# The second stream of batches runs half a period behind the first in the last stage of a four-stage network

## The chip, the cores and the metric

The kernel runs on one core of one Trainium2 chip. The metric is device time in microseconds of the whole program. Engines are named as in the profile: PE (TensorE, its weight loads are PEld), DVE (VectorE), ACT (ScalarE), POOL (GpSimd), SP (the queue that issues most transfers).

## The reference

Four blocks follow one another on an activation of 4 batches x 1024 tokens x 128 channels: a Mamba block, a top-2 mixture of experts, a differential attention, and a last block, which the change touches. The last block normalizes twice, gates 8 attention experts, sums their q, k and v projections weighted by the gate, makes one causal attention of it, projects with 8 weighted output matrices, normalizes, gates 8 experts of a second mixture, and normalizes once more:

```python
logits = normalize(flat_hs) @ normalize(sim) - sigmoid(gates)   # then mask and softmax: weight of each of 8 experts
q, k, v = sum over e of w_e * (h @ q_proj[e]), w_e * (h @ k_proj[e]), w_e * (h @ v_proj[e])
h = h + sum over e of w_e * (softmax(causal(q k^T)) v @ o_proj[e])
h = h + sum over e of m_e * (gelu(layernorm(h) @ w1[e]) @ w2[e])
```

Each block's output is layer-normalized and added to its input. (The lines above are shortened from the reference; E = 8, hidden size 128.)

## The kernel before

Each engine has one instruction queue that it works through in order. Work of different batches is interleaved when the program is written out: every part is a Python generator that yields a due time ahead of each piece, and `weave` always takes the stream with the smallest due time. The due times (tables `D_LN`, `D_TR`, `D_GATE`, `D_ATT`, `D_OUT`, `D_MOE` with `D_PERIOD` and `D_EXPERT`) never reach the chip; they only fix the order in each queue. What really holds an instruction back are semaphores.

The last stage has two streams. Stream k = 0 does batches 0 and 2, stream k = 1 batches 1 and 3; each has its own PSUM banks (stream 0 has `ps0` and `ps1`, stream 1 has `ps2` and `ps3`) and its own buffers. Before the change both streams have the same due times, so that every piece of stream 1 stands right behind the same piece of stream 0. One batch (index r in a stream) goes through these parts, with due times from the start of its period of 177.2:

- **Normalizations and first gate** (0 to 24). `stats` (8 x BN_STATS, 8 x BN_AGGR on DVE), `rstd` on POOL, `norms` on DVE, the same again with `affine`; transposes on PE, copies to `xT` on ACT, `logits` on PE (L1586), gate arithmetic on DVE (L1323 to L1347), an exponential on ACT (L1506), the weights on DVE (L1352 to L1358).
- **Projection steps** q = 0..15 (24 to 76). POOL scales the tile (L1476), PE transposes it (L1597), ACT and DVE split it into a high and a low half (L1521, L1380), PE multiplies with q and k weights (L645 to L647, six products of 512 columns) and with the v weights (L1648, 12 products). Behind step 7 and step 15 ACT copies q, k and v out (L1526 to L1529).
- **Attention rows** i = 0..7 (76 to 110). PE scores (L1608), DVE mask and maximum (L1394, L1396), ACT exponential (L1536), PE transposes (L1668), ACT copies (L1544), PE output (L1678), DVE scaling by the row's sum (L1386, piece `weighed`). The scores of row i + 1 wait for the exponential of row i.
- **Head steps** j = 0..7 (111 to 126). Two PE products of 512 columns (L1696), then eight additions in a chain on DVE (L1410).
- **Second normalization and gate** (125 to 142), as above.
- **Expert steps** x = 0..15 (142 to 171). PE up (L1711), ACT Gelu (L1557), PE down (L1724), DVE four additions (L1430).
- **Last normalization** (171 to 177), its sum into `X` on POOL (L1484), and the store.

Ahead of both streams stand `experts_act`, `experts_dve`, `experts_pool` and `experts_pe`: they prepare the gate matrices and split the q, k and v weights, loaded in this stage as `raw`, into two fp16 halves (three copies on ACT at L1267, three subtractions on DVE at L1285).

Of the kernel before, what the change touches and what calls it, by code (L numbers as in the profile page):

```python
# [104 lines left out]
def program(nc, d, out):  # L105
    ctx = ExitStack()
    with ctx:
# [1078 lines left out]
        D_PERIOD, D_EXPERT = 177.2, 3.15  # L1186
# [6 lines left out]
        def d_at(r, t):  # L1193
            return D_PERIOD * r + t

        def d_scaled(r, q):

            h, x = q // 8, q % 8
            return d_at(r, 24 + 26.2 * h if x == 0 else 25 + 26.2 * h + D_EXPERT * (x - 1))

        def d_proj(r, q, more=0.0):
            return d_at(r, 25 + 26.2 * (q // 8) + D_EXPERT * (q % 8) + more)
# [57 lines left out]
        def experts_act(e):  # L1260
            e.wait_ge(phase, 8)
            e.wait_ge(*t_dsp.at(0))
            e.activation(lsq[:, 16:32], bank[0][:, 0:16], ACT.Copy, scale=1.0).then_inc(*a_dsp.up("sq"))
            e.activation(flat(sgm[:, :, :]), flat(gts[:, :, :]), ACT.Exp, bias=0.0, scale=-1.0).then_inc(*a_dsp.up("exp"))
            e.wait_ge(s_wq, 16)
# [4 lines left out]
        def experts_dve(e):  # L1270
            e.wait_ge(phase, 8)
# [4 lines left out]
            e.reciprocal(sgm[:, :, :], sgm[:, :, :]).then_inc(*v_dsp.up("sgm"))  # L1276
            e.wait_ge(*p_dsp.at(0))
# [5 lines left out]
            for a in range(3):  # L1283
                e.wait_ge(*a_dsp.at(a))
                e.scalar_tensor_tensor(out=flat(wqkv3[:, 1, a, :, :]), in0=raw[:, 1024 * a:1024 * a + 1024], scalar=WS,  # L1285
                                       in1=flat(wqkv3[:, 0, a, :, :]), op0=ALU.mult, op1=ALU.subtract).then_inc(*v_dsp.up(a))

        def experts_pool(e):
            e.wait_ge(phase, 8)
# [3 lines left out]
        def experts_pe(e):  # L1293
            e.wait_ge(phase, 8)
# [3 lines left out]
        def soft_dve(e, k):  # L1298
# [17 lines left out]
            def gating(r, w, times):  # L1316
                which = w // 2
                yield d_at(r, times[1])
                e.wait_ge(*p_dln[k].at(r, w, "sq"))
                e.tensor_reduce(G(7)[:, :, 0:1], s_sq[k], AX, ALU.add).then_inc(*v_dgt[k].up(r, w, "sumsq"))  # L1320
                yield d_at(r, times[2])
# [27 lines left out]
                yield d_at(r, times[3])  # L1349
# [11 lines left out]
            for r in range(2):  # L1361
                b = k + 2 * r
                yield d_at(r, D_LN[0][0])
                stats(e, s, [tile_of(b, j) for j in range(8)], {}).then_inc(*v_dln[k].up(r, 0, "stats"))
                yield d_at(r, D_LN[0][1])
                e.wait_ge(*p_dln[k].at(r, 0, "rstd"))
                norms(e, s, [tile_of(b, j) for j in range(8)], hs).then_inc(*v_dln[k].up(r, 0, "out"))
                yield d_at(r, D_LN[1][0])
                stats(e, s, hst, {0: v_dln[k].at(r, 0, "out")}).then_inc(*v_dln[k].up(r, 1, "stats"))
                yield d_at(r, D_LN[1][1])  # L1370
# [5 lines left out]
                for q in range(16):  # L1376
                    yield d_scaled(r, q)
# [12 lines left out]
                for i in range(8):  # L1390
                    yield d_at(r, D_ATT[i])
# [8 lines left out]
                    yield d_at(r, D_ATT[i] + 1.5)  # L1400
# [3 lines left out]
                yield d_at(r, D_ATT[8])  # L1404
                weighed(7)
                for j in range(8):
                    yield d_at(r, D_OUT + 1.8 * (j + 1))
# [8 lines left out]
                yield d_at(r, D_LN[2][0])  # L1416
                stats(e, s, hst, {0: v_dom[k].at(r, 7)}).then_inc(*v_dln[k].up(r, 2, "stats"))
                yield d_at(r, D_LN[2][1])
# [3 lines left out]
                for x in range(16):  # L1422
                    yield d_at(r, D_MOE + 1.6 * (x + 2))
# [10 lines left out]
                yield d_at(r, D_LN[3][0])  # L1434
                stats(e, s, hst, {0: v_dm[k].at(r, 15)}).then_inc(*v_dln[k].up(r, 3, "stats"))
                yield d_at(r, D_LN[3][1])
# [5 lines left out]
        def soft_pool(e, k):  # L1442
# [9 lines left out]
            for r in range(2):  # L1452
                b = k + 2 * r
                yield d_at(r, D_LN[0][0])
                root(r, 0)
                for w in (0, 2):
                    yield d_at(r, D_LN[w // 2 + 1][0])
                    root(r, w // 2 + 1)
                    yield d_at(r, D_GATE[w // 2][0])
                    e.wait_ge(*v_dln[k].at(r, w // 2 + 1, "out"))  # L1460
                    e.tensor_tensor(s_sq[k], n1, n1, ALU.mult).then_inc(*p_dln[k].up(r, w, "sq"))
                    yield d_at(r, D_GATE[w // 2][2])
# [4 lines left out]
                    for q in range(16):  # L1467
                        h, x = q // 8, q % 8
                        yield d_scaled(r, q)
# [9 lines left out]
                yield d_at(r, D_LN[3][0])  # L1479
                root(r, 3)  # L1480
                yield d_at(r, D_LN[3][1])
# [4 lines left out]
        def soft_act(e, k):  # L1486
# [21 lines left out]
            for r in range(2):  # L1508
                yield d_at(r, D_TR[0])
                turned(r, 0)  # L1510
                yield d_at(r, D_GATE[0][2])
                gate(r, 0)
                for q in range(16):
                    h = q // 8
                    yield d_scaled(r, q)
# [6 lines left out]
                    if q % 8 == 7:  # L1522
                        yield d_proj(r, q, D_EXPERT)
# [7 lines left out]
                for i in range(8):  # L1531
                    yield d_at(r, D_ATT[i])
# [5 lines left out]
                    yield d_at(r, D_ATT[i] + 1.5)  # L1538
# [7 lines left out]
                yield d_at(r, D_TR[1])  # L1546
                turned(r, 1)
                yield d_at(r, D_TR[2])
                turned(r, 2)
                yield d_at(r, D_GATE[1][2])  # L1550
                gate(r, 2)
                for x in range(16):
                    yield d_at(r, D_MOE + 1.6 * x)
# [5 lines left out]
        def soft_pe(e, k):  # L1559
# [51 lines left out]
            for r in range(2):  # L1611
                yield d_at(r, D_TR[0])
                turn(r, 0)
                yield d_at(r, D_GATE[0][2])
                logits(r, 0)
                for q in range(16):
                    h, x = q // 8, q % 8
                    if x == 0:
                        yield d_scaled(r, q)
                        scaled(r, q)  # L1620
                    yield d_proj(r, q)
# [228 lines left out]
```

## Time and profile before

| | |
|---|---|
| Median of 3 runs | 3174.92 us (3171.91 to 3175.52) |
| The profiled execution: its time, its span | 3170.2 us, 3168.4 us |
| Busy share of the span: PE, DVE, ACT, POOL | 76%, 73%, 53%, 40% |
| Last stage (first instruction on DVE to the end of the last sum into X) | 2500.8 to 3160.1 us |
| Mean granted TensorE clock | 0.866 |

The span is the profiled part of an execution. The last stage is the last fifth of it, and its two periods (r = 0 and r = 1) repeat each other. A granted clock of 1.00 is 2.4 GHz and 0.50 is 1.2 GHz.

### The profile page before, as it was taken

The numbers are of one execution on the slowest core, as the hardware profiler recorded it, in microseconds if no ns is written. First come the engines' busy times: TensorE is split into PE (matmuls) and PEld (weight loads), VectorE is DVE, ScalarE is ACT, GpSimd is POOL, SyncE is SP. The second block draws the span as 40 slices with busy tenths as digits, with TensorE's granted clock in tenths as the row PEclk, the third lists the DMA queues.
The fourth block names the chain that finished last, engine by engine and source line by source line (L and its number), as shares of the span: only waits on it lengthen the run. The fifth ranks groups of instructions, "written<-read, shape, count | busy, mean of one in ns | idle before, by whom it ended". The sixth has DMA issues, their size and how long they took to land.

```text
span 3168.4 us, 41094 instructions
## 1 busy us (share of the span) xinstructions
PE 2407.0 (76%) x14962; PEld 1690.2 (53%) x14962; DVE 2311.8 (73%) x4141; ACT 1678.5 (53%) x2552; POOL 1263.5 (40%) x1203
## 2 busy tenths in 40 slices
PE   3114776667676696899999999999999388667867
PEld 1002444344344564577777777776777366245635
DVE  3994798699599612688878878887888533874386
ACT  4223663665376242678777877787778124022402
POOL 0341143144124200365766576667667540114011
PEclk8556878888788898799999999999999789788978
DMA  3000000000000000100000100010000100000000
GB/s 99 0 0 0 0 1 1 1 1 1 1 1 1 1 1 14 41 21 21 24 21 21 28 21 21 24 29 21 21 21 1 40 1 1 0 14 1 1 0 14
DMA packets 32026, 41.96 MB, mean 13 GB/s; under 512 B 8897, under 2 KB 18130, under 8 KB 31442
## 3 DMA queue, kind: packets, MB, share of 16 engines
q1 hardware_dynamic: 31826, 39.34, 4.6%
q8 instruction: 120, 1.97, 0.3%
q14 instruction: 80, 0.66, 0.1%
HBM read 12.05 MB, written 2.10 MB: 4 GB/s over the span
## 4 chain that ended last, share of the span: by engine, by line
PE 46%; DVE 20%; issue 18%; POOL 11%; ACT 4%; SPq 1%; DMA 1%; POOLq 0%; DVEq 0%; ACTq 0%
PE ps L954 10%; PE ps L932 6%; PE ps L943 6%; POOL MA L379 5%; PE ps L710 3%; DVE MA L1090 3%; DVE MA L1410 3%; PE ps L914 2%; DVE lnb L265 2%; PE ps L1724 2%; PE ps L645 2%; PE ps L1711 2%; PE ps L647 1%; PE ps L646 1%; PE ps L1648 1%
## 5 line engine op out<-in xcount | busy, mean ns | idle before, releaser
L1090 DVE TENSOR_REDUCE MA<-ps 128x1 f32<-128x1024 f32 x512 | 623.1, 1220 | 190.4 <-PE ps L932 177.6
L379 POOL TENSOR_TENSOR MA<-MA,BIG 128x1024 f32<-128x1024 f32 x120 | 280.1, 2355 | 624.3 <-DVE BIG L350 624.3
L954 PE MATMUL ps<-MA,WB 128*64 128x128 f32 x4096 | 504.5, 277 | 0.0
L954 PEld LDWEIGHTS ps<-MA,WB 128*64 128x64 f32 x4096 | 442.8, 137 | 88.4 <-issue 87.4
L344 DVE TENSOR_TENSOR_SCAN BIG<-BIG 128x1024 f32<-128x1024 f32 x128 | 346.8, 2748 | 0.0
L932 PE MATMUL ps<-BIG 96*128 96x512 f16 x1024 | 312.6, 387 | 13.3 <-DMA BIG<-WB 4.9
L632 ACT ACTIVATE HR<-ps,b 128x512 f32<-128x512 f32 x288 | 191.5, 686 | 244.0 <-PE ps L647 243.0
L710 PEld LDWEIGHTS ps<-WB,HR 128*128 128x128 f32 x2304 | 305.8, 209 | 25.0 <-issue 8.7
L710 PE MATMUL ps<-WB,HR 128*128 128x128 f32 x2304 | 312.8, 294 | 0.0
L1017 ACT ACTIVATE WB<-ps,MA 128x1024 f32<-128x1024 f32 x206 | 229.5, 1114 | 149.3 <-DVE MA L1090 147.5
L497 PE MATMUL ps<-bc,sel 96*128 96x512 bf16 x256 | 108.2, 520 | 249.1 <-DVE BIG L350 190.7
L1024 ACT ACTIVATE MA<-ps 128x1024 f32<-128x1024 f32 x256 | 259.8, 1015 | 4.9 <-PE ps L943 4.9
L436 ACT ACTIVATE BIG<-MA,aneg 128x1024 f32<-128x1024 f32 x128 | 141.5, 1142 | 109.9 <-DVE BIG L344 105.8
L1017 ACT ACTIVATE MA<-ps,MA 128x1024 f32<-128x1024 f32 x153 | 170.6, 1115 | 44.8 <-DVE MA L1090 44.8
L497 PEld LDWEIGHTS ps<-bc,sel 96*128 96x128 bf16 x256 | 22.2, 113 | 302.2 <-DVE BIG L350 213.0
L1147 POOL TENSOR_TENSOR MA<-MA 128x2 f32<-128x2 f32 x128 | 25.0, 195 | 365.2 <-DVE MA L1094 365.2
L943 PE MATMUL ps<-ident,WB 128*128 128x128 f32 x1232 | 166.1, 279 | 5.6 <-POOL WB L1159 2.5
L943 PEld LDWEIGHTS ps<-ident,WB 128*128 128x128 f32 x1232 | 144.4, 144 | 44.4 <-DVE WB L1099 10.8
L645 PE MATMUL ps<-xT,WB 128*128 128x512 f16 x288 | 126.5, 439 | 52.4 <-ACT HR L632 48.3
L248 POOL TENSOR_SCALAR st_d<-st_d 128x8 f32<-128x8 f32 x16 | 4.3, 269 | 402.6 <-DVE st_d L260 402.5
L589 DVE SCALAR_TENSOR_TENSOR acc<-ps,g,acc 128x128 f32<-128x128 f32 x256 | 71.0, 337 | 123.2 <-PE ps L710 123.2
L340 DVE TENSOR_TENSOR BIG<-MA,ps 128x1024 f32<-128x1024 f32 x128 | 149.6, 1207 | 1.2 <-PE ps L497 1.2
(286 smaller groups left out, 5133.2 us busy)
## 6 DMA issues: line engine op xcount, KB each, us to landing
BIG<-BIG SPq DMA_DIRECT2D x192, 64.0 KB, 2.0
BIG<-WB SPq DMA_DIRECT2D x192, 64.0 KB, 2.0
WB<-w_dram SPq DMA_DIRECT2D x1, 2304.0 KB, 14.6
X<-x_dram SPq DMA_DIRECT2D x4, 512.0 KB, 12.5
HR<-w_dram SPq DMA_DIRECT2D x1, 2048.0 KB, 9.3
out_dram<-X SPq DMA_DIRECT2D x4, 512.0 KB, 3.2
WB<-wqkv_dram SPq DMA_DIRECT2D x1, 1536.0 KB, 6.1
WB<-w_dram SPq DMA_DIRECT2D x2, 512.0 KB, 8.2
```

Of the source, the lines that this page charges most:

```text
L340: e.tensor_tensor(db[k][c], du[:, c, :], ps[0][:, :], ALU.mult).then_inc(*v_mtb.up(b, n, c))
L344: e.tensor_tensor_scan(db[k][c], da[k][c], db[k][c], 0.0, ALU.mult, ALU.add).then_inc(*v_mscan.up(b, n, c))
L379: e.tensor_tensor(yy[:, c, :], yy[:, c, :], db[n % 2][c], ALU.add).then_inc(*p_my.up(b, n, c))
L632: e.activation(hr[(4 * k + f) % 8], bank[4 + f % 2], ACT.Gelu, bias=small["b1"][:, PLAN[k][1], f:f + 1], scale=BACK).then_inc(*a_fg.up(b, ...
L645: e.matmul(o, w[0], x[0], start=first, stop=False)
L710: i = e.matmul(o, hr[(4 * kk + f) % 8][:, 128 * j:128 * j + 128], w2[:, x, f, :], start=f == 0 and x != 8, stop=f == 3)
L932: x = e.matmul(ps[s][:, 512 * h:512 * h + 512], stack[q % 2][0:96, 0, 2 * pp + s, 128 * i:128 * i + 128], stack[q % 2][0:96, 1, 2 * pp + s ...
L943: x = e.transpose(ps[2][:, 128 * k:128 * k + 128], P_of(n, 0)[:, 128 * k:128 * k + 128], ident[:, :])
L954: x = e.matmul(bank[6][64 * pp:64 * pp + 64, 0:128], V[(4 * b + g) % 2][:, k, 64 * pp:64 * pp + 64], DT[n % 2][:, 128 * k:128 * k + 128], ...
L1017: e.activation(P_of(n, s), ps[s][:, :], ACT.Exp, bias=L[:, 2 * s + pp:2 * s + pp + 1], scale=1.0, accum_out=L[:, 4 + 2 * s + pp:5 + 2 * s ...
L1024: e.activation(DT[n % 2], ps[2][:, :], ACT.Copy, scale=1.0).then_inc(*a_at.up(n))
L1090: e.tensor_reduce(L_of(n)[:, c:c + 1], ps[s][:, :], AX, ALU.max, negate=True).then_inc(*v_amx.up(n, s))
```

## The change

Stream 1 gets a shift `D_SHIFT` = 88.0 on all its due times, about half of the period of 177.2. Its first half (normalizations, projections) now stands among the second half (attention rows, head steps, experts) of a batch of stream 0, and the other way round. The `experts_*` functions become streams of their own with due times: the gate preparation stands partly behind the first statistics, and the three weight splits of DVE stand at 13.2, 16.7 and 20.2. No instruction of the computation is added or removed; only the order in the queues changes. (ACT table loads are placed by the compiler where the function's table changes in the queue.)

```diff
-        D_PERIOD, D_EXPERT = 177.2, 3.15
+        D_PERIOD, D_EXPERT, D_SHIFT = 177.2, 3.15, 88.0
...
-        def d_at(r, t):
-            return D_PERIOD * r + t
+        def d_at(k, r, t):
+            return D_PERIOD * r + D_SHIFT * k + t
...
         def experts_dve(e):
-            e.wait_ge(phase, 8)
+            yield 0.2
             e.tensor_tensor(lsq[:, 0:16], sims, sims, ALU.mult).then_inc(*v_dsp.up("sq"))
...
             e.reciprocal(sgm[:, :, :], sgm[:, :, :]).then_inc(*v_dsp.up("sgm"))
+            yield 7.5
             e.wait_ge(*p_dsp.at(0))
...
             for a in range(3):
+                yield 13.2 + 3.5 * a
                 e.wait_ge(*a_dsp.at(a))
...
-            experts_dve(e)
-            weave(soft_dve(e, 0), soft_dve(e, 1))
+            e.wait_ge(phase, 8)
+            weave(experts_dve(e), soft_dve(e, 0), soft_dve(e, 1))
```

The other engines change in the same way (`experts_act` yields 0.3 and 8.5, `experts_pool` 6.0, `experts_pe` 0.3), and every `d_at`, `d_scaled` and `d_proj` gets the stream's k. Line numbers behind L1183 rise by up to 3: L1380, L1410, L1506 and L1557 of before are L1383, L1413, L1509 and L1560 after the change.

On DVE, at the start of the stage, the queue before the change is this (L1278 to L1282 prepare the gate matrix, L1285 are the splits, `st_d0` and `st_d1` are the statistics of the two streams):

```order
L1272 TENSOR_TENSOR lsq<-sims 128x16
L1274 TENSOR_SCALAR sgm<-sgm 128x16
L1276 RECIPROCAL sgm<-sgm 128x16
L1278 TENSOR_SCALAR lsq<-lsq 128x16
L1280 RECIPROCAL lsq<-lsq 128x16
L1282 TENSOR_TENSOR simn<-sims,lsq 128x16
L1285 SCALAR_TENSOR_TENSOR WB<-WB 128x1024 x3
L256 BN_STATS st_d0<-X 128x6 x8
L260 BN_AGGR st_d0<-st_d0 128x2 x8
L256 BN_STATS st_d1<-X 128x6 x8
```

and after it this:

```order
L256 BN_STATS st_d0<-MA 128x6 x8
L260 BN_AGGR st_d0<-st_d0 128x2 x8
L1280 TENSOR_SCALAR lsq<-lsq 128x16
L1282 RECIPROCAL lsq<-lsq 128x16
L1284 TENSOR_TENSOR simn<-sims,lsq 128x16
L265 TENSOR_SCALAR MA<-MA,st_d0 128x128 x8
L1313 TENSOR_TENSOR MA<-MA,lnp 128x1024
L1316 TENSOR_TENSOR MA<-MA,lnp 128x1024
L1288 SCALAR_TENSOR_TENSOR WB<-WB 128x1024
L1323 TENSOR_REDUCE BIG<-BIG 128x8
L1288 SCALAR_TENSOR_TENSOR WB<-WB 128x1024
L1326 TENSOR_SCALAR BIG<-BIG 128x8
```

Only stream 0 starts here now; the gate preparation stands between its second statistics and its second normalization, and the splits (L1288) stand between pieces of its gate.

On DVE, around the second normalization, the queue before has the head steps of both streams in turn (L1410), then both statistics:

```order
L1410 SCALAR_TENSOR_TENSOR MA<-ps2,BIG,MA 128x128 x8
L1410 SCALAR_TENSOR_TENSOR MA<-ps1,BIG,MA 128x128 x8
L256 BN_STATS st_d0<-MA 128x6 x8
L260 BN_AGGR st_d0<-st_d0 128x2 x8
L1410 SCALAR_TENSOR_TENSOR MA<-ps3,BIG,MA 128x128 x8
L256 BN_STATS st_d1<-MA 128x6 x8
```

After the change, here in the part where stream 1 does its second half and stream 0 its first, the same place reads:

```order
L1413 SCALAR_TENSOR_TENSOR MA<-ps2,BIG,MA 128x128 x8
L1383 SCALAR_TENSOR_TENSOR BIG<-ps1,BIG 128x512
L1413 SCALAR_TENSOR_TENSOR MA<-ps3,BIG,MA 128x128 x8
L256 BN_STATS st_d1<-MA 128x6 x8
L260 BN_AGGR st_d1<-st_d1 128x2 x8
L1383 SCALAR_TENSOR_TENSOR BIG<-ps1,BIG 128x512
L265 TENSOR_SCALAR MA<-MA,st_d1 128x128 x8
L1313 TENSOR_TENSOR MA<-MA,lnp 128x1024
L1316 TENSOR_TENSOR MA<-MA,lnp 128x1024
L1383 SCALAR_TENSOR_TENSOR BIG<-ps1,BIG 128x512 x2
L1323 TENSOR_REDUCE BIG<-BIG 128x8
```

The low halves of stream 0's projection steps (L1383) now stand between stream 1's head steps and behind its normalization blocks.

On ACT, the queue before goes from the copies of the last projection step to the attention rows of both streams, with no table load between them:

```order
L1526 ACTIVATE MA<-ps0 128x512
L1527 ACTIVATE MA<-ps0 128x512
L1529 ACTIVATE MA<-ps1 128x512
L1536 ACTIVATE WB,BIG<-ps0,BIG 128x128
L1526 ACTIVATE MA<-ps2 128x512
L1527 ACTIVATE MA<-ps2 128x512
L1529 ACTIVATE MA<-ps3 128x512
L1536 ACTIVATE WB,BIG<-ps2,BIG 128x128
```

After the change, at the end of stream 0's expert steps (L1560, Gelu) and the start of stream 1's rows (L1539, the exponential):

```order
L1560 ACTIVATE HR<-ps0 128x512 x4
L1529 ACTIVATE MA<-ps2 128x512
L1530 ACTIVATE MA<-ps2 128x512
L1532 ACTIVATE MA<-ps3 128x512
L1539 ACT_TABLE_LOAD
L1539 ACTIVATE WB,BIG<-ps2,BIG 128x128
L1560 ACT_TABLE_LOAD
L1560 ACTIVATE HR<-ps0 128x512
L1547 ACTIVATE BIG<-ps3 128x128
L1560 ACTIVATE HR<-ps0 128x512
L1539 ACT_TABLE_LOAD
L1539 ACTIVATE WB,BIG<-ps2,BIG 128x256
```

The tail of one stream's Gelus is now mixed with the first two exponentials of the other, with three table loads among them; the whole stage has 13 table loads after the change, where it had 3.

## Rows read from the trace of the kernel before

**Rows 1.** The page's first line.

```profile
span 3168.4 us, 41094 instructions
```

**Rows 2.** Chain that ended last, by time: start us, length us, what.

```profile
2500.77 6.12 DMA WB<-wqkv_dram
2506.91 1.06 ACT WB L1267
2508.00 3.49 DVE WB L1285 x3
2511.49 1.57 DVE st_d L256 x8
...
2555.18 0.43 PE ps L645
```

**Rows 3.** Same chain: period, expert steps, last sum.

```profile
2737.86 1.66 DVE st_d L256 x8
...
3100.50 1.78 PE ps L1724 x16
...
3104.00 1.78 PE ps L1724 x16
...
3157.77 2.34 POOL X L1484
```

**Rows 4.** Busy time in stretches: PE, PEld, DVE, ACT, POOL (xinstructions), clock, DMA, GB/s.

```profile
2832.00:3157.00 325.00, 239.55 (x1464) 164.22 (x1464) 197.62 (x732) 78.39 (x150) 68.16 (x59) 0.85 0.01 4
...
2884.00:2964.00 80.00, 75.64 (x690) 52.94 (x688) 21.20 (x34) 23.58 (x45) 26.02 (x25) 1.00 0.01 1
2964.00:3012.00 48.00, 41.09 (x250) 30.62 (x251) 20.86 (x58) 23.24 (x54) 0.00 (x0) 1.00 0.00 1
3012.00:3066.00 54.00, 36.55 (x90) 14.86 (x88) 44.80 (x142) 2.06 (x4) 1.34 (x2) 0.89 0.00 0
3066.00:3096.00 30.00, 16.96 (x56) 12.52 (x56) 26.35 (x127) 4.11 (x7) 9.53 (x7) 0.52 0.00 0
3096.00:3146.00 50.00, 49.27 (x282) 35.88 (x283) 30.46 (x114) 18.28 (x32) 0.00 (x0) 1.00 0.00 1
```

**Rows 5.** Timeline, second normalization and gate: start, length, instruction, idle before.

```profile
3062.17 1.64 DVE L256 BATCH_NORM_STATS2 st_d<-MA 128x6 f32<-128x128 f32 x8
...
3064.91 1.68 POOL L250 TENSOR_TENSOR st_d<-st_d,half 128x8 f32<-128x8 f32 x1
...
3069.70 2.11 DVE L265 TENSOR_SCALAR MA<-MA,st_d 128x128 f32<-128x128 f32 x8
...
3073.10 1.23 DVE L1313 TENSOR_TENSOR MA<-MA,lnp 128x1024 f32<-128x1024 f32 x1
...
3082.29 6.83 PE L1586 MATMUL ps<-simn,xT 128*128 128x8 f32 x32
...
3085.82 0.22 DVE L1328 TENSOR_TENSOR BIG<-ps,BIG 128x64 f32<-128x64 f32 x1 [1.32 <-PE ps L1586]
...
3089.75 0.22 DVE L1347 TENSOR_TENSOR BIG<-BIG 128x64 f32<-128x64 f32 x1
...
3094.78 1.28 ACT L1557 ACT_TABLE_LOAD   x1
```

**Rows 6.** Groups by line and shape, 2832 to 3157 us: busy us, mean ns.

```profile
L1380 DVE SCALAR_TENSOR_TENSOR BIG<-ps,BIG 128x512 f16<-128x512 f32 x32 | 22.0, 691 | 54.4 <-ACT BIG L1521 54.4
L1521 ACT ACTIVATE BIG<-ps 128x512 f16<-128x512 f32 x32 | 19.0, 600 | 50.6 <-PE ps L1597 50.6
...
L265 DVE TENSOR_SCALAR lnb<-MA,st_d 128x128 f32<-128x128 f32 x20 | 7.4, 440 | 0.1
...
L1536 ACT ACTIVATE WB<-ps,BIG 128x1024 f32<-128x1024 f32 x2 | 2.2, 1110 | 1.8 <-DVE BIG L1396 1.8
```

**Rows 7.** Timeline, first head steps of the second period.

```profile
3014.62 8.11 PE L1696 MATMUL ps<-WB,xT 128*128 128x512 f32 x18
...
3017.63 12.58 DVE L1410 SCALAR_TENSOR_TENSOR MA<-ps,BIG,MA 128x128 f32<-128x128 f32 x34 [4.23 <-PE ps L1696]
```

More of the change, by code:

```diff
@@ L1191, in program, with d_scaled, d_proj @@
         D_OUT, D_MOE = 111, 142.4
-        def d_at(r, t):
-            return D_PERIOD * r + t
-        def d_scaled(r, q):
+        def d_at(k, r, t):
+            return D_PERIOD * r + D_SHIFT * k + t
+        def d_scaled(k, r, q):
             h, x = q // 8, q % 8
-            return d_at(r, 24 + 26.2 * h if x == 0 else 25 + 26.2 * h + D_EXPERT * (x - 1))
-        def d_proj(r, q, more=0.0):
-            return d_at(r, 25 + 26.2 * (q // 8) + D_EXPERT * (q % 8) + more)
+            return d_at(k, r, 24 + 26.2 * h if x == 0 else 25 + 26.2 * h + D_EXPERT * (x - 1))
+        def d_proj(k, r, q, more=0.0):
+            return d_at(k, r, 25 + 26.2 * (q // 8) + D_EXPERT * (q % 8) + more)
         def parts(i):
@@ L1260, in experts_act @@
         def experts_act(e):
-            e.wait_ge(phase, 8)
+            yield 0.3
             e.wait_ge(*t_dsp.at(0))
@@ L1317, in gating @@
                 which = w // 2
-                yield d_at(r, times[1])
+                yield d_at(k, r, times[1])
                 e.wait_ge(*p_dln[k].at(r, w, "sq"))
                 e.tensor_reduce(G(7)[:, :, 0:1], s_sq[k], AX, ALU.add).then_inc(*v_dgt[k].up(r, w, "sumsq"))
-                yield d_at(r, times[2])
+                yield d_at(k, r, times[2])
                 e.wait_ge(*p_dln[k].at(r, w, "norm"))
@@ L1348, in gating @@
                     *v_dgt[k].up(r, w, "pre"))
-                yield d_at(r, times[3])
+                yield d_at(k, r, times[3])
                 e.wait_ge(*a_dtr[k].at(r, w, "exp"))
@@ L1508, in soft_act @@
             for r in range(2):
-                yield d_at(r, D_TR[0])
+                yield d_at(k, r, D_TR[0])
                 turned(r, 0)
-                yield d_at(r, D_GATE[0][2])
+                yield d_at(k, r, D_GATE[0][2])
                 gate(r, 0)
@@ L1611, in soft_pe @@
             for r in range(2):
-                yield d_at(r, D_TR[0])
+                yield d_at(k, r, D_TR[0])
                 turn(r, 0)
-                yield d_at(r, D_GATE[0][2])
+                yield d_at(k, r, D_GATE[0][2])
                 logits(r, 0)
@@ L1618, in soft_pe @@
                     if x == 0:
-                        yield d_scaled(r, q)
+                        yield d_scaled(k, r, q)
                         scaled(r, q)
-                    yield d_proj(r, q)
+                    yield d_proj(k, r, q)
                     if x < 7:
@@ L1766, in _ @@
             e.drain().then_inc(phase, 1)
-            experts_act(e)
-            weave(soft_act(e, 0), soft_act(e, 1))
+            e.wait_ge(phase, 8)
+            weave(experts_act(e), soft_act(e, 0), soft_act(e, 1))
         @block.vector
@@ L1786, in _ @@
             e.drain().then_inc(phase, 1)
-            experts_pool(e)
-            weave(soft_pool(e, 0), soft_pool(e, 1))
+            e.wait_ge(phase, 8)
+            weave(experts_pool(e), soft_pool(e, 0), soft_pool(e, 1))
         @block.sync
```

90 lines of the change are left out of this document (45 added, 45 removed).

## Prediction

> **What bounds the kernel now.** I read the page's first line, then the chain of waits through the last stage, then the busy times stretch by stretch, then the timeline of single pieces. The change touches nothing ahead of 2500.8 us, so only the last stage counts: from there to the end of the last sum into X at 3157.77 + 2.34 = 3160.1 it takes 659.3 us of a span of 3168.4 [rows 1 to 3]. It is a start of about 11 us (the weight load, the ACT copy and the three DVE splits lie on the chain ahead of the first statistics at 2511.5), two periods of 3062.17 - 2737.86 = 324.3 us [rows 3, 5], and nothing else; 10.7 + 2 x 324.3 = 659.3.
>
> Inside a period the bound changes. The reader should see in the stretches [rows 4]: the projection steps (80 us) are PE's, 75.64 us busy for 32 steps of both streams, so 2.36 us of PE a step; the expert steps are PE's too, 3.50 us for a pair, 1.75 a step [rows 3]; the head steps (54 us) are DVE's with PE at two thirds; the normalization and gate (30 us) are a chain over DVE, POOL, PE and ACT with the clock at 0.52. PE has 239.55 us of work in 325. So there is room: 85 us of idle PE a period.
>
> **The change, part by part.** Let T be the stage's new length. With half a period of shift the queues hold five half periods: the first half of a batch of stream 0 alone, three in which the second half of one batch (I call it the late one) stands beside the first half of another (the early one), and the second half of stream 1's last batch alone. T = first + 3 m + last. Before, a first and a second half of one batch together cost 324.3 / 2 = 162 us; m is what they cost when they come from different streams.
>
> *First, alone.* Statistics are 2.3 us (1.64 + 0.64), the POOL root with its addition 2.0, a normalization 2.1, scale and bias 1.2 each [rows 5]. One stream needs 2.3 + 2.0 + 2.1 + 2.3 + 2.0 + 2.1 + 2.5 = 15.4 us to the end of its second normalization. The gate preparation now stands in the middle of it: its POOL power queues behind the root and DVE waits, about 3.7 us (three short DVE pieces and a power on 16 columns; twice the 1.68 us of the 8-column one is taken). Transposes and copy take 3.5, the logits of one stream 6.83 / 2 = 3.4 at low clock, the gate 3089.97 - 3085.82 = 4.2, the last split 1.2, the weights 1.1, the first scaled tile to the first product 4.4: first product at 37 us, against 2555.18 - 2500.77 = 54.4 before [rows 2, 5]. Of the splits two hide behind POOL and PE. Then 16 steps of 2.4, 1.6 for the copies behind step 7, 1 for the slow clock, and about 9 for the copies and rows 0 to 3: **87**.
>
> *Last, alone.* Rows 4 to 7 about 21 (each a loop of scores, 128-column steps of maximum, an exponential of up to 1.11 us [rows 6]; 48 us for 16 rows of both streams is the nearest row [rows 4]); transposes, copy and first head product 4.2; eight head steps of 12.58 x 8 / 34 = 2.96, 23.7 [rows 7]; normalization, gate and first Gelu 22; 16 x 1.75 = 28; last additions 2; last normalization with its eight writes of 0.44 and the POOL sum 10.3 [rows 3, 6]; 3 for the low clock: **114**.
>
> *Three mixed halves, m.* Each queue is in order, so a piece that waits holds the other stream's pieces behind it. I follow the queues with the durations above.
> A. Late rows 4 to 7 beside early normalizations and gate. DVE does statistics 1.3 to 3.6, row 4, normalization to 8.4, statistics to 10.8, row 5, the POOL root to 13.0, scale and bias to 17.7, row 6 to 19.1; ACT must first copy xT (19.7), exponential 6 to 21.1, scores 7 1.7, row 7's maximum to 24.3, exponential, transposes, copies and output to 29.2; the logits stand behind that on PE (30.9), the gate on DVE to 35.1, and only then `weighed` 7, transposes, copy, first head product: 39.2.
> B. Seven late head steps 20.8, four early low halves (L1380) of 0.69 among them 2.8 [rows 6], one handover PE to ACT to DVE 1.9: 25.7. Here PE gets 4 to 5 projection steps done for nothing.
> C. Late second normalization and gate beside early steps 5 to 8. Head step 7 and statistics 5.3, root 7.4, normalization, scale and bias 12.1: PE stands at the late transposes for 4 us with steps behind it. Low halves, step 6, 7, reduction, root and logits to 19.4; gate to 23.6. ACT has the gate's exponential queued ahead of the early q, k, v copies and of step 8's high half, so these start only at 23.9: 1.9 + 0.6 + 0.7, then step 8: 29.6. PE idles another 7 us.
> D. Expert steps 0 to 13 beside early steps 9 to 15: 14 x 1.75 + 7 x 2.36 = 41, and 0.5 for the first Gelu: 41.5. This is PE's work at its full rate, the same as before.
> E. Late experts 14 and 15 and last normalization beside early rows 0 to 3. The chain is copies 1.9, a table load 1.3, exponential 0, load, Gelu 15, load, exponential 1, the late additions, statistics, root, normalization, row 3: 20.5.
> Sum 39.2 + 25.7 + 29.6 + 41.5 + 20.5 = **156.5**. The same walk with the due times of the first and third mixed halves (1.2 apart) gives 155.
>
> *The table loads.* The load takes 1.28 us and the Gelu behind it follows at once [rows 5]; of 10 more loads in the queue the six beside the first two exponentials of E count, already in the 20.5, about 2.6 us a half on the chain. The Trainium skill (ScalarE: Activation LUTs, What ACT_TABLE_LOAD costs) gives about 2.66 us for a switch, with a drain; by that the three handovers would cost some 8 us more in all. The trace here shows no such drain, and the sum does not use it.
>
> *The clock.* [...] At 0.50 each scores or logits piece on the chain doubles: 7 us in A, 4 in C, 3 at the start of D, 14 at most. I take a third of it, 4.5. The other bound is 0. m = 160.
>
> T = 87 + 3 x 160 + 114 = 681, 22 us above 659.3. The profiled execution took 3170.2; its span and what lies around the stage stay. 3170.2 + 22 = 3192, and as the median of the runs is 4.7 us above that execution, **3197**. The level from which it decides is m = (659.3 - 201) / 3 = 152.8: each microsecond of m is three of the time.
>
> **Why a rearrangement with so much idle PE may lose.** The half alone at each end costs 201 us for work that cost 162 before, 39 more; the start gives 11 back by itself (it is in the 87); the mixed halves must save 13 each to pay, of a PE floor far below (107 us at full clock: 38 for projections, 20 for rows, 14 for head steps, 28 for experts, 7 for transposes and logits). Only B really overlaps two bounds. In A and C the late and the early chain both go through DVE (27 us of work in A's 39), and E is a chain.
>
> **Rivals.**
> - *The streams fill each other's gaps.* For it: PE 239.55 of 325 us busy [rows 4], and each half alone is a chain (87 and 114) shorter than the floor needs. If the waits in A and C were hidden and m came to 130, T = 591 and the time 3107. Milder, m = 145 (C's two stalls, 11 us, gone): 636, 3152. It decides below 152.8. Against it: the order of the pieces, above.
> - *It cancels.* m from 151 to 155: within 6 us of the time before, some 3175.
> - *The clock stays low in A, C and E.* All of the 14 us, m = 170: T = 711, 3227. For it: the clock 0.52 in the normalization stretch, against it: 1.00 with PE at two thirds in most of the head steps. The Trainium skill (TensorE: Matmul & The Clock Gate, What's actually happening) has the idle array throttled by default and released by activity, which is the direction of this rival.
> - *Only the start pays and the shift is neutral*: m = 149, 3164; it is counted with the milder form of the first.
>
> **How the numbers follow.** Chances: my forecast (m 155 to 166) 0.42; clock or coupling worse (m above 166) 0.20; cancels 0.12; gaps partly filled (m 140 to 151) 0.18; filled well (below 140) 0.08. A measurement here tells about 0.2%, 6 us, from no change. Slower by more than that 0.63, same 0.11, faster 0.26. The range leaves out the well-filled case and the extreme of the low clock: 3145 to 3238; the likeliest case alone is 3182 to 3215.
>
> **What would show it.** In the profile after: the stage starts its first product 37 us behind 2500.8, not 54; the distance between two head-step blocks of the two streams is some 157 to 160 us (the mixed half), not near 130; PE idle for 4 us at the late transposes and for 7 us behind the late logits; table loads in pairs at each handover; a clock below 1.00 in A and C. Wrong would be a mixed half below 153, most likely because a wait that I put on the chain in A (logits behind the late output, xT copy ahead of exponential 6) had slack, or above 166, if the clock stays down or the steps' handovers over four engines cost more than I gave them.

## The result, and the profile after

The changed kernel takes 3212.57 us (median of 4 runs, 3208.77 to 3214.94) against 3174.85 (4 runs, 3171.91 to 3175.52): a ratio of 1.0119, with a 95% interval of 1.0102 to 1.0137. It is 37.7 us slower; 22 were forecast. The profiled execution took 3212.93.

The page's first line, for [rows 1]:

```profile
span 3211.1 us, 41104 instructions
```

Where [rows 2] has the first product of the projections at 2555.18, PE's timeline now has it at 2539.54 (start us, length us, instruction, idle before):

```profile
2536.04 1.12 PE L1600 MATMUL ps<-ident,BIG 128*128 128x128 f32 x4 [8.33 <-POOL BIG L1479]
2539.54 0.63 PE L645 MATMUL ps<-BIG,WB 128*128 128x512 f16 x1
```

The last stage starts at 2502.15, so this is 37.4 us into it. The maxima of attention row 3 (512 columns) stand where the terms of the sum meet: the first half ends with the first of them, each mixed half with the next. In DVE's timeline:

```profile
2591.97 0.69 DVE L1399 TENSOR_REDUCE BIG<-ps 128x1 f32<-128x512 f32 x1
...
2757.58 0.69 DVE L1399 TENSOR_REDUCE BIG<-ps 128x1 f32<-128x512 f32 x1
...
2925.43 0.69 DVE L1399 TENSOR_REDUCE BIG<-ps 128x1 f32<-128x512 f32 x1
...
3092.09 0.69 DVE L1399 TENSOR_REDUCE BIG<-ps 128x1 f32<-128x512 f32 x1
```

The sum into X of the last batch, which ends the stage, for the last row of [rows 3]:

```profile
3204.80 2.34 POOL L1487 TENSOR_TENSOR X<-X,lnb 128x1024 f32<-128x1024 f32 x1 [2.25 <-DVE lnb L265]
```

That gives the terms of the sum: first half 2592.66 - 2502.15 = 90.5 us, mixed halves 165.6, 167.9 and 166.7, last half 3207.14 - 3092.78 = 114.4; together 705.0. For the kernel before, the timeline shows a sum that the chain of waits doesn't name:

```profile
3157.77 2.34 POOL L1484 TENSOR_TENSOR X<-X,lnb 128x1024 f32<-128x1024 f32 x1
3160.14 4.67 SPq L1742 DMA_DIRECT2D out_dram<-X  x2
3162.07 2.34 POOL L1484 TENSOR_TENSOR X<-X,lnb 128x1024 f32<-128x1024 f32 x1 [1.96 <-DVE lnb L265]
```

The chain's last sum is the one at 3157.77; behind it stands only a piece of POOL's own queue:

```profile
3162.03 2.37 POOLq L107
```

The other stream's sum, at the same place in time, ends at 3164.4. The stage before took 663.6 us, not 659.3; it grew by 41.4, and 1.4 us came in ahead of it, which makes the 42.7 us between the two spans.

The mixed half in sections, from the view of busy time in stretches (columns as in [rows 4]); A, B, C, then D with E, then the other two mixed halves:

```profile
2593.00:2639.00 46.00, 30.62 (x155) 21.52 (x154) 25.42 (x115) 12.08 (x25) 10.49 (x9) 0.85 0.00 1
2639.00:2663.00 24.00, 22.04 (x114) 11.39 (x114) 21.74 (x62) 2.39 (x4) 2.10 (x2) 1.00 0.00 1
2663.00:2702.00 39.00, 21.53 (x140) 14.46 (x141) 19.57 (x82) 5.75 (x12) 12.62 (x12) 0.74 0.00 1
2702.00:2758.00 56.00, 50.66 (x332) 35.90 (x330) 29.57 (x107) 22.30 (x38) 6.67 (x7) 0.98 0.00 1
2758.00:2926.00 168.00, 128.30 (x733) 84.73 (x732) 97.14 (x365) 42.83 (x78) 33.80 (x30) 0.86 0.01 4
2926.00:3092.00 166.00, 127.59 (x733) 84.51 (x732) 95.94 (x364) 42.84 (x78) 32.92 (x30) 0.87 0.01 4
```

In B and in D with E, PE is 90% busy or more, as planned. A and C are where PE stands: 15 us idle of 46, 17 of 39, at a granted clock of 0.85 and 0.74.

What made PE wait in the last stage (engine, line, waited for: total us, times, longest us), after:

```profile
PE ps L1600 <- POOL BIG L1479: 38.5, 7, 8.8
PE ps L1577 <- DVE MA L1316: 30.5, 4, 16.2
PE ps L1611 <- ACT WB L1539: 29.2, 15, 5.5
PE ps L1600 <- DVE BIG L1383: 26.1, 8, 7.0
```

Before, most of PE's waiting was for the normalization:

```profile
PE ps L1574 <- DVE MA L1313: 107.7, 8, 30.3
```

It shrank to 30.5 us, and 29.3 of these are two waits in the halves that run alone (16.21 before the transposes at 2521.47, 13.08 before those at 3155.60). In the mixed halves it is all but gone. But three other waits appeared: for the scaled tile, for the exponential of the row before (L1611 for L1539), and for the low half (L1600 for L1383). Here is the longest, in section C, from the timeline of all engines:

```profile
2667.31 0.64 DVE L260 BATCH_NORM_AGGREGATE st_d<-st_d 128x2 f32<-128x6 f32 x8
2668.04 0.25 POOL L248 TENSOR_SCALAR st_d<-st_d 128x8 f32<-128x8 f32 x1 [21.91 <-DVE st_d L260]
2668.37 1.67 POOL L250 TENSOR_TENSOR st_d<-st_d,half 128x8 f32<-128x8 f32 x1
2670.01 2.05 POOL L1479 TENSOR_TENSOR BIG<-MA,BIG 128x512 f32<-128x512 f32 x2
2671.11 0.71 PEld L1600 LDWEIGHTS ps<-ident,BIG 128*128 128x128 f32 x4 [9.61 <-POOL BIG L1479]
2671.11 1.11 PE L1600 MATMUL ps<-ident,BIG 128*128 128x128 f32 x4 [8.78 <-POOL BIG L1479]
```

POOL idles for 21.91 us at the late stream's root (L248 and L250), because the late stream's statistics aren't there yet. The early stream's scaled tile, which needs only buffers, stands behind that root in the queue, and PE waits 8.78 us for it. The Trainium skill (Perfetto Trace Analysis, Tensor Engine Instruction) has DVE, ACT and GpSimd as strictly first in, first out. The trace agrees: POOL starts the tile only behind the root, after 21.91 us of idle time.

### The profile page after: what moved, and what is told of

Its sections match the earlier page's. It is cut to its first block, busy times and chain, and to the rows that moved or that the text cites. A ratio compares the mean times of both kernels' runs of the same rounds, so it can differ in the third digit from the quotient of the medians.

```text
span 3211.1 us, 41104 instructions
## 1 busy us (share of the span) xinstructions
PE 2441.9 (76%) x14962; PEld 1702.3 (53%) x14962; DVE 2306.3 (72%) x4141; ACT 1691.8 (53%) x2562; POOL 1264.0 (39%) x1203
## 4 chain that ended last, share of the span: by engine, by line
PE 45%; DVE 20%; issue 18%; POOL 11%; ACT 5%; SPq 1%; DMA 0%; POOLq 0%; DVEq 0%; ACTq 0%
PE ps L954 10%; PE ps L932 6%; PE ps L943 5%; POOL MA L379 4%; DVE MA L1090 3%; PE ps L710 3%; DVE MA L1413 2%; PE ps L914 2%; PE ps L1714 2%; PE ps L1727 2%; DVE lnb L265 2%; PE ps L645 1%; PE ps L647 1%; PE ps L646 1%; PE ps L1611 1%
## 5 line engine op out<-in xcount | busy, mean ns | idle before, releaser
L943 PEld LDWEIGHTS ps<-ident,WB 128*128 128x128 f32 x1232 | 143.5, 143 | 45.0 <-DVE WB L1099 10.3
L1383 DVE SCALAR_TENSOR_TENSOR BIG<-ps,BIG 128x512 f16<-128x512 f32 x64 | 44.2, 690 | 137.6 <-ACT BIG L1524 137.6
```

The lines of the kernel that those rows point to most:

```text
L943: x = e.transpose(ps[2][:, 128 * k:128 * k + 128], P_of(n, 0)[:, 128 * k:128 * k + 128], ident[:, :])
```

## The experiments

The expectations name two theories. H: the loss lies in pieces of one stream that stand in an in-order queue behind a piece of the other stream that is still waiting. G: the loss lies in what the streams share (engines, PE's clock), whatever the order.

**1. The splits alone.** `D_SHIFT` is 0; the `experts_*` streams stay woven in.

```diff
-        D_PERIOD, D_EXPERT, D_SHIFT = 177.2, 3.15, 88.0
+        D_PERIOD, D_EXPERT, D_SHIFT = 177.2, 3.15, 0.0
```

> The streams of batches stay together (shift 0); only the gate preparation and the weight splits are woven in behind the first statistics. Both theories: it shortens the start only. The 10.7 us ahead of the first statistics go, but DVE is full in the first normalizations of two streams, so the three splits (1.2 us each) and the wait for the 2.9 us power on POOL come back: 4 to 8 us faster than before, about 3169 us. If the start were hidden anyway: no change, 3175.

3169.3 us (3166.9 to 3173.4); ratio 0.9989, interval 0.9980 to 0.9998. With the streams side by side, the woven start is worth about 4 us.

**2. The shift alone.** `experts_*` run to their end ahead of both streams, on all four engines.

```diff
-            weave(experts_pe(e), soft_pe(e, 0), soft_pe(e, 1))
+            weave(experts_pe(e))
+            weave(soft_pe(e, 0), soft_pe(e, 1))
```

> The shift of 88 alone; gate preparation and splits stand ahead of both streams as before the change. The shift is the whole loss: slower than the changed kernel by what the start gives back to one stream alone, 10.7 less 2.9 + 0.7 (power and its three short pieces) less 1.2 (last split) = 6 us: about 3218 us. If the woven splits were what costs: near 3175.

3218.36 us (3215.2 to 3220.8); ratio 1.0144, interval 1.0128 to 1.0159. The loss is the shift's; the start gives back 6 us of it (by the medians; 8 by the two ratios).

**3. The POOL root behind one more scaled tile.**

```diff
-                    yield d_at(k, r, D_LN[w // 2 + 1][0])
+                    yield d_at(k, r, D_LN[w // 2 + 1][0] + w)
                     root(r, w // 2 + 1)
```

> The changed kernel, with one order changed on POOL: the root of the second normalization stands 2 due units later, behind the next scaled tile of the other stream. Theory H (a piece that waits in an in-order queue holds the other stream): PE's idle time of 8.8 us at the late head steps' end falls to some 3 us in each of three mixed halves, 3 to 5 us of it on the chain, so 9 to 15 us faster than the changed kernel, about 3200 us. Rival G (the mixed halves are long because the work of both streams contends for DVE and PE and the clock is low; order does not matter): no change, 3212.

3203.35 us (3201.3 to 3205.7); ratio 1.0092, interval 1.0078 to 1.0105: 9 us back. PE's total wait for scaled tiles fell from 38.5 to 29.4 us, in step with the time.

**4. Due times stretched to what the trace shows.** The due times say 177.2 for a period that lasts over 300 us, so a constant shift in them is not a constant shift in time. Here every table is stretched in the same manner, those of the gates, the rows and the `experts_*` too, and the exponentials of both gates come later on ACT. The diff is shortened.

```diff
-        D_PERIOD, D_EXPERT, D_SHIFT = 177.2, 3.15, 88.0
+        D_PERIOD, D_EXPERT, D_SHIFT = 262, 5.2, 131
...
-        D_LN = [(0, 3), (5, 8), (125.4, 128.4), (171.2, 174.2)]
+        D_LN = [(0, 4.5), (6.7, 11), (183, 187.5), (255, 259.5)]
...
-        D_OUT, D_MOE = 111, 142.4
+        D_OUT, D_MOE = 156.5, 200.5
...
-                yield d_at(k, r, D_GATE[1][2])
+                yield d_at(k, r, D_GATE[1][3] - 0.1)
                 gate(r, 2)
```

> The shift with all due times stretched to what the pieces took in the changed kernel (period 262, shift 131, head step 3.3, projection step 5.2, expert step 3.25, normalizations at their real distances; the gate's exponential on ACT queued where its input is ready). Theory H: pieces stand where they become ready, the mixed halves fall from 166 to 135 to 142 us, so 70 to 90 us faster than the changed kernel and about 3125 to 3145. Rival G: within 15 us of the changed kernel, 3197 or more.

3189.54 us (3186.9 to 3190.8); ratio 1.0048, interval 1.0034 to 1.0061. It is 23 us better than the change, but 45 to 65 us short of what H expected. The same POOL root still stood ahead of the scaled tile:

```profile
2822.24 0.25 POOL L248 TENSOR_SCALAR st_d<-st_d 128x8 f32<-128x8 f32 x1 [16.60 <-DVE st_d L260]
...
2825.30 1.11 PE L1600 MATMUL ps<-ident,BIG 128*128 128x128 f32 x4 [7.86 <-POOL BIG L1479]
```

**5. Three orders, on the change as it is.** POOL's scaled tiles go 3.0 earlier in its queue, the exponentials of both gates on ACT go later (the second gate's lands behind the other stream's q, k, v copies and high halves), and `weighed(7)` on DVE goes earlier, ahead of the other stream's gate: `D_ATT[8]` is 110.0 and `D_ATT[7] + 1.8` is 106.9.

```diff
-                        yield d_scaled(k, r, q)
+                        yield d_scaled(k, r, q) - 3.0
...
-                yield d_at(k, r, D_GATE[0][2])
+                yield d_at(k, r, D_GATE[0][3] - 0.1)
                 gate(r, 0)
...
-                yield d_at(k, r, D_GATE[1][2])
+                yield d_at(k, r, D_GATE[1][3] + 0.6)
                 gate(r, 2)
...
-                yield d_at(k, r, D_ATT[8])
+                yield d_at(k, r, D_ATT[7] + 1.8)
                 weighed(7)
```

> The changed kernel with three orders changed and nothing else: on POOL each scaled tile stands 3 due units earlier (ahead of the other stream's root); on ACT the second gate's exponential stands behind the other stream's q, k, v copies and its next high half; on DVE the scaling of the last attention row stands ahead of the other stream's gate. Theory H: each takes one named wait off the chain of each of three mixed halves: some 3 us for the POOL one (9 in all measured in its simpler form), 2.5 for the ACT one, 2.7 for the DVE one, so about 24 us faster than the changed kernel, 3188 us. Rival G (contention and clock, order does not matter beyond POOL's): 3203 or more.

3186.0 us (3183.6 to 3191.0); ratio 1.0045, interval 1.0032 to 1.0058. 27 us come back by order alone (by the medians; 23 by the two ratios).

**6 and 7. A shift of 30, without and with the first two orders** (the edits of 5 on POOL and on ACT; the diff shows the shift alone).

```diff
-        D_PERIOD, D_EXPERT, D_SHIFT = 177.2, 3.15, 88.0
+        D_PERIOD, D_EXPERT, D_SHIFT = 177.2, 3.15, 30.0
```

> The changed kernel with D_SHIFT = 30 in place of 88. One stream's projection steps (PE) then stand beside the other's normalization or rows, and one's head steps (DVE) beside the other's expert steps (PE), while only about 30 due units of a batch are alone at each end. Theory H': the tail of a stream alone is what the shift of 88 loses (201 us of first and last half for work of 162 before), so a smaller shift loses less: ends cost 35 to 45 us, the two periods 290 to 310 each: 3150 to 3175. Rival: what matters is that the streams' pieces interleave in any other order than side by side, each mismatch of due times with real times costing waits: 3190 or more.

> As e6, with POOL's scaled tiles 3 due units earlier and the second gate's exponential on ACT behind the copies. Theory H: faster than e6 by 4 to 12 us, since a waiting root or exponential again holds the other stream's pieces. Rival G: equal to e6 within 3 us.

3194.29 us (3192.9 to 3196.6), ratio 1.0068 (1.0055 to 1.0081), and 3168.81 us (3166.9 to 3178.3), ratio 0.9996 (0.9987 to 1.0005). Even a third of the shift costs 22 us, and the two orders take 25.5 back (23 by the two ratios), where I had expected 4 to 12.

What the two orders move here isn't what they move in kernel 5. At a shift of 30 nothing of the other stream stands between the old and the new place of the second gate's exponential, so it stays where it was: ACT idles 4.9 to 5.4 us for it in both kernels. What moves is the first gate's, behind the other stream's copies. In ACT's timeline, kernel 6 and then kernel 7, where the last of these copies (L1532) comes at 2576.09, ahead of it:

```profile
2581.43 0.26 ACT L1509 ACTIVATE BIG<-BIG 128x64 f32<-128x64 f32 x1 [9.37 <-DVE BIG L1350]
```

```profile
2581.78 0.26 ACT L1509 ACTIVATE BIG<-BIG 128x64 f32<-128x64 f32 x1 [3.17 <-DVE BIG L1350]
```

PE's wait for scaled tiles falls from 38.1 to 20.9 us, and the stage has 7 table loads for 9. At this shift the loss lies in the order of the queues. That the size of the shift costs nothing doesn't follow: kernel 5, with a shift of 88 and these orders and one more, still takes 3186.0.

**8. One switch of tables a handover.** Period 183.0, shift 91.5: the same expert and row pieces meet at other due times, and the stage has 7 table loads in place of 13.

```diff
-        D_PERIOD, D_EXPERT, D_SHIFT = 177.2, 3.15, 88.0
+        D_PERIOD, D_EXPERT, D_SHIFT = 183.0, 3.15, 91.5
```

> The changed kernel with D_PERIOD 183.0 and D_SHIFT 91.5, so that all Gelus of a batch stand ahead of the other stream's exponentials: 7 table loads in the stage where there were 13. If the loads are on the chain as predicted, two loads of 1.28 us fewer at each of three handovers: 7 to 8 us faster than the changed kernel, 3205. If they hide behind the other stream: 3212 within 3 us. The period alone shifts each second half by 2.9 to 3.5 due units, which may give or cost some us of its own.

3218.84 us (3216.9 to 3219.4); ratio 1.0146, interval 1.0131 to 1.0161: slower than the change. The new due times also moved other pieces (PE's waits for exponentials rose from 29.2 to 37.8 us, those for head steps from 10.3 to 23.4), so this run doesn't price the loads; it only shows that six fewer of them bring nothing that outweighs such a shuffle.

**9. Three orders without a shift.** The edits of 5, with `D_SHIFT` 0.

> No shift (as the splits-only kernel, 3169.3), with the three orders: POOL's scaled tiles 3.0 earlier in its queue, the gates' exponential on ACT later, weighed(7) later on DVE. Theory H (the orders pay because they take one stream's piece from behind the other stream's wait, which needs two streams at different places): with equal due times nothing stands in between, so 3169, between 3164 and 3174. Rival G (the orders are better in themselves, whatever the shift): 3142 to 3150, since they gave 27 us at a shift of 88.

3170.48 us (3166.2 to 3173.1); ratio 0.9987, interval 0.9978 to 0.9996, the same as kernel 1. But this run tests less than I meant it to. With equal due times in both streams the new ones lead `weave` through the pieces in the same order on all four engines, so its queues are those of kernel 1, and its waits on PE are too (101.4 us for the normalization, 16.5 for head steps, 16.3 for scaled tiles in both). It is a second measurement of kernel 1. It bears out H's remark that with no shift nothing stands in between; whether the orders would be a gain in themselves it can't say. `weighed(7)` went earlier here too, not later.

**10. Three orders, shift 15.** The edits of 5, with `D_SHIFT` 15.0.

> Shift of 15 with the three orders. Theory H: the second stream's normalizations stand beside the first's gate and first steps, and row 0 to 7 of the two streams stay beside each other; the half alone at each end shrinks to 15 us of work. Without the blocked pieces it should be at or a little below the kernel without a shift: 3150 to 3168. Rival G (any shift costs, since the pieces of the two streams contend for DVE and the clock falls): the cost is in proportion to the shift, so 3169 + 15/88 of the 17 us that are left at 88, 3172.

3176.17 us (3168.7 to 3180.0); ratio 1.0010, interval 1.0001 to 1.0019. Both theories missed. The rows show one block: the second stream's first tile waits on POOL for its gate (6.73 us) with the first stream's next tile behind it:

```profile
2557.15 2.05 POOL L1479 TENSOR_TENSOR BIG<-MA,BIG 128x512 f32<-128x512 f32 x2 [6.73 <-DVE BIG L1361]
```

The orders didn't make it: all tiles go 3.0 earlier together, so at a shift of 15 these two stand in this order with and without the edits. The profiled execution took 3168.69, the shortest of the 11, so the rows don't show what the median has on top.

**11. Shift 30 with the third order too.** Kernel 7 and the `weighed(7)` edit of 5.

> Shift of 30 with all three orders; the kernel with two of them took 3168.8. Theory H: weighed(7) frees the rows of the one stream from behind the other's gate; at a shift of 88 three orders gave 27 us, at 30 two of them gave 25.5, and the third is worth 0 to 6 here: 3163 to 3169. Rival G: no change, 3168 to 3171.

3182.11 us (3176.2 to 3188.7); ratio 1.0024, interval 1.0015 to 1.0033: 13 us slower than kernel 7 by the medians, 9 by the two ratios, where both expectations had no loss. This is the most telling miss. Stretch 2502 to 3215, first kernel 7, then kernel 11:

```profile
2502.00:3215.00 713.00, 494.68 (x2930) 333.04 (x2930) 394.09 (x1465) 165.81 (x308) 140.93 (x118) 0.88 0.02 8
```

```profile
2502.00:3215.00 713.00, 511.69 (x2930) 344.63 (x2930) 395.08 (x1465) 165.29 (x308) 139.44 (x118) 0.85 0.02 8
```

PE has the same 2,930 products in both, and 17.0 us more of busy time in the second, at a granted clock of 0.85 and not 0.88. Kernel 11's last sum ends 17.1 us later in these profiles (3182.9 and 3165.8), so PE's idle time from 2502 on is the same: 169 us.

The edit puts `weighed(7)` earlier in DVE's queue, for stream 1 ahead of the other stream's gate arithmetic. That is the fault that H names, made anew. DVE idles for PE's last output of the row with the gate behind it, the gate's exponential comes late on ACT, and the copies of the turned tile stand behind that:

```profile
2745.69 0.35 DVE L1389 TENSOR_SCALAR MA<-ps,BIG 128x128 f32<-128x128 f32 x1 [6.21 <-PE ps L1681]
...
2750.59 0.26 ACT L1509 ACTIVATE BIG<-BIG 128x64 f32<-128x64 f32 x1 [9.16 <-DVE BIG L1350]
...
2751.87 3.78 PE L1699 MATMUL ps<-WB,xT 128*128 128x512 f32 x4 [4.99 <-ACT xT L1505]
```

In kernel 7, DVE does the gate in that time, with `weighed(7)` behind it, and ACT waits 5.34 us in place of 9.16. Over the stage, kernel 11 has these waits on PE:

```profile
PE ps L1699 <- ACT xT L1505: 11.6, 4, 5.1
```

Kernel 7 has 2.7 us there. Kernel 5 has 11.7 (the change itself 2.7), from the same three waits (6.57 on DVE, 9.50 on ACT, 5.11 on PE), so this third order probably cost something in it too; it wasn't run apart there. That the moved waits are what lowers the clock on the work behind them is the likeliest reading of the 17 us, but no run sets the clock by itself.

**12. Stretched due times, orders changed again.** Kernel 4 with scaled tiles 4.0 earlier, the second gate's exponential 0.7 later on ACT, and `weighed(7)` at `D_ATT[7] + 2.6`. That last due time is 2.9 ahead of the old one and leaves DVE's queue as it was; the exponential is the edit that the expectation doesn't name, and it lands behind the other stream's copies and next high half.

```diff
-                        yield d_scaled(k, r, q)
+                        yield d_scaled(k, r, q) - 4.0
...
-                yield d_at(k, r, D_GATE[1][3] - 0.1)
+                yield d_at(k, r, D_GATE[1][3] + 0.6)
                 gate(r, 2)
```

> The kernel with the stretched due times (period 262, shift 131; 3189.5), in which PE still waited 7.9 us for a scaled tile behind the POOL root; now POOL's scaled tiles stand 4.0 earlier and weighed(7) 2.6 later. Theory H: the mixed half loses a wait of 5 to 8 us three times, 3166 to 3178. Rival G (the waits only move to the next handover, contention bounds the mixed half): 3183 to 3190.

3169.93 us (3165.8 to 3171.4); ratio 0.9986, interval 0.9977 to 0.9995: 19.6 us better than kernel 4, inside H's range and outside G's. PE's waits for low halves fell from 24.8 to 11.4 us, those for scaled tiles from 38.7 to 33.0, so by the waits the greater part goes with ACT's order; the edits weren't run apart. Its mixed halves are 153.1, 153.6 and 153.5 us, from these rows:

```profile
2587.87 0.69 DVE L1399 TENSOR_REDUCE BIG<-ps 128x1 f32<-128x512 f32 x1
...
2740.92 0.69 DVE L1399 TENSOR_REDUCE BIG<-ps 128x1 f32<-128x512 f32 x1
...
2894.48 0.69 DVE L1399 TENSOR_REDUCE BIG<-ps 128x1 f32<-128x512 f32 x1
...
3048.01 0.69 DVE L1399 TENSOR_REDUCE BIG<-ps 128x1 f32<-128x512 f32 x1
```

The forecast's level from which it decides was 152.8; with the stage's right end, kernel 12's later start (2502.02 for 2500.77) and its two ends (86.5 and 115.3) it is (663.6 - 1.2 - 201.8) / 3 = 153.5. The kernel sits on it, and its span is 3168.0 us for the 3168.4 of before. Kernels 1, 9 and 12 have the lowest ratios and kernel 7 the lowest median, and none is clearly past 0.2%; no version found beats both kernels by an amount worth having.

## Why it came out as it did

**Where the 42.7 us went, on PE.** PE's busy time in the last stage, from the same view, before and after:

```profile
2502.00:3215.00 713.00, 481.46 (x2928) 329.71 (x2928) 398.32 (x1464) 158.53 (x303) 137.82 (x117) 0.85 0.02 8
```

```profile
2502.00:3215.00 713.00, 511.55 (x2930) 338.95 (x2930) 392.81 (x1465) 171.23 (x314) 139.44 (x118) 0.85 0.02 8
```

30.1 us of the 42.7 are the same products taking longer (29.5 if the two products between 2500.77 and 2502 are counted in before); idle time (end of the last sum, less 2502, less busy) went from 180.9 to 193.6, up 12.7. The mean granted clock is 0.85 in both, and that misleads. Before, the low clock fell mostly on stretches in which PE had nothing to do; after, it falls on work. Taking PE's busy time in stretches of 6 us, each weighted by its clock, I get a clock while busy of 0.92 before and 0.89 after. By that, 511.5 us of busy time would have been 495 at the old clock: some 16 of the 30 us. The same sum for kernels 7 and 11 gives 0.91 and 0.88, and 511.7 x 0.88 / 0.91 = 495, so there the clock is about all of the difference in busy time. The other 14 us here are not settled; PE's ends are modelled, and busy time is the union of overlapping records. The scores of 512 columns show it most, 48 of them before and 48 after:

```profile
L1608 PE MATMUL ps<-MA 128*128 128x512 f32 x48 | 24.5, 605 | 0.0
```

```profile
L1611 PE MATMUL ps<-MA 128*128 128x512 f32 x48 | 32.2, 773 | 26.9 <-ACT WB L1539 26.9
```

The same view of kernel 12 has 504.50 us busy; its stage ends at 3164.0, so PE idles 157.5 us there, 23 less than before. The shift did fill the gaps in that order, and 23 us more of busy time took it back.

**The forecast's steps, one by one.**

- *Start.* First product after 37.4 us, 37 forecast: right. The first half took 90.5 for 87.
- *Last half.* 114.4 for 114: right.
- *The length before.* I read the end of the stage off the chain, at 3160.1; it was 3164.4. The change had 4.3 us less to lose than my sum said. This error helped the forecast, since 681 less 663.6 is 17, not 22. So did the 4.7 us that I added for the distance from the profiled execution to the median: the change's profiled execution lies within 0.4 us of its median, and in the profiled executions the miss is 21 us (3212.93 for 3192), not 16.
- *A, forecast 39.2, measured 46.1* (2592.66 to the first head addition at 2638.75). Two blocks that I had walked past. Row 4's maximum stands behind the early stream's first normalization, and this behind its POOL root: PE has row 4's scores done, and DVE idles for the root (2.09 us) with them behind it. In the timeline:

```profile
2593.59 1.28 PE L1611 MATMUL ps<-MA 128*128 128x512 f32 x4
...
2598.50 2.14 DVE L265 TENSOR_SCALAR MA<-X,st_d 128x128 f32<-128x128 f32 x8 [2.09 <-POOL st_d L250]
2600.56 0.29 DVE L1397 TENSOR_TENSOR ps<-ps,tri 128x128 f32<-128x128 f32 x1
...
2601.74 0.80 ACT L1539 ACTIVATE WB<-ps,BIG 128x640 f32<-128x640 f32 x1 [5.80 <-DVE BIG L1399]
...
2602.68 2.93 PE L1611 MATMUL ps<-MA 128*128 128x512 f32 x4 [5.53 <-ACT WB L1539]
```

  The products of scores 5 (768 columns, those of scores 4 have 640) take 2.93 us at 2602.68: a wait of 5.53 us, then a granted clock of 0.50 from 2602.6 to 2605.7. In the next half the same products take half of that, at 1.00:

```profile
2764.18 1.46 PE L1611 MATMUL ps<-MA 128*128 128x512 f32 x4
```

  And the first head addition stands behind the early stream's low half, which waits 5.95 us:

```profile
2638.14 0.69 DVE L1383 SCALAR_TENSOR_TENSOR BIG<-ps,BIG 128x512 f16<-128x512 f32 x1 [5.95 <-ACT BIG L1524]
2638.75 1.50 DVE L1413 SCALAR_TENSOR_TENSOR MA<-ps,BIG,MA 128x128 f32<-128x128 f32 x4
```

- *B, forecast 25.7, measured 24.* Right.
- *C, forecast 29.6, measured 39* (2663 to the first expert product at 2702.37). The step that failed is "PE stands at the late transposes for 4 us with steps behind it". At the late transposes PE waits 0.60 us (2678.20, and 0.60 and nothing in the other two mixed halves). What it stands for is a scaled tile behind POOL's root: 8.78 us here, then 1.88 for the next one; kernel 3, which only moves that tile ahead of the root, is 9 us faster. I had asked of PE and DVE what was queued behind what, and not of POOL. The other stall was as forecast, "PE idles another 7 us": 6.88, behind the gate's exponential on ACT, which idles 10.42 and has the copies and the next high half queued behind it.

```profile
2693.34 0.26 ACT L1509 ACTIVATE BIG<-BIG 128x64 f32<-128x64 f32 x1 [10.42 <-DVE BIG L1350]
...
2694.94 0.61 ACT L1524 ACTIVATE BIG<-ps 128x512 f16<-128x512 f32 x1
...
2696.42 0.87 PE L1600 MATMUL ps<-ident,BIG 128*128 128x128 f32 x3 [6.88 <-DVE BIG L1383]
```

- *D and E, forecast 62, measured 56.* Too much: the expert steps and the rows at the handover overlap more than my chain allowed. The three table loads of the handover are in it, at 2743.05, 2744.82 and 2747.39, 1.28 us each with the next function right behind.
- *The clock, 4.5 of a possible 14 a half.* The mixed halves came to 165.6, 167.9 and 166.7 for 160, so the sum was 20 us short in three halves. In this half A and C ran 16.7 over my walk; D and E gave 6 of it back, which was luck and no part of the reasoning. How much of this is clock and how much wait can't be split cleanly here; between kernels 7 and 11, PE's busy time differs by 17 us in one stage. My case against a low clock was weaker than I wrote it: [rows 4] has the head steps at 0.89, not at 1.00.
- *Slips in the sums.* The start adds up to 15.3, not 15.4, B to 25.5, not 25.7. "The mixed halves must save 13 each" leaves out the 11 us of the start; 162 less the level of 152.8 is 9 each.

**The balance.** A plain half cost 324.3 / 2 = 162 us before. The two halves alone cost 204.9 for work worth 162, so 43 more; the mixed halves cost 4.5 more each, 14 together, where they had to save 9 each; the old start (11) and the 4.3 between the two last sums come off: 41.

**The rivals.** *The gaps are filled* is half right: kernel 12 gets there in idle time, and it is then even with the kernel before and no better. *Only the start pays and the shift is neutral* is what kernel 7 shows, after two queues were put in order. *The clock stays low* was the right direction; m, at 166.7 on average, lies just inside that case, while the time, 3212.57, lies in the range of the likeliest one. That both fit is due to the two errors named under *the length before*.

## What to carry to other kernels

When two streams are woven into in-order queues with an offset, list for every engine, the slow helper too, each instruction that waits for a chain of its own stream, and ask what of the other stream stands behind it; two such places (POOL's roots, ACT's gate exponentials) were worth 25 us in kernel 7 and 20 in kernel 12, and one piece put the wrong side of another stream's gate cost 13 (9 by the ratios) in kernel 11. Read the queues after an edit of due times, too: here two moved nothing (kernel 9, `weighed(7)` in kernel 12) and one moved another piece than the one meant (kernel 7). Before that, price the two ends, where one stream runs alone: the mixed parts have to save that much, shared among them, before anything is won. And compare PE's busy time for the same products, not the mean granted clock: it shows whether low clock falls on idle time or on work.

## What was not expected of the hardware

Moving one short DVE piece up in its queue changed PE's busy time by 17 us of 495 for the same instructions (kernels 7 and 11), with 8.9 us more of waiting for the turned tile and no more idle time in all. The Trainium skill (TensorE: Matmul & The Clock Gate, What's actually happening) has the array throttled unless activity releases it; the trace agrees in direction: scores 5 take 2.93 us at a granted clock of 0.50 behind a wait of 5.53 (2602.68), and 1.46 at 1.00 where PE was at work before them (2764.18).
